# A softmax attention kernel: the place of small side matmuls within a key block is changed

## What is computed

```python
# layer 1: softmax attention, 16 heads of width 16, on n = layernorm(x)
q = n * rotation ; k = n * entangle ; v = n          # per head
out = softmax(q k^T / 4) v                            # 2048 x 2048 scores per head, 4*16 = 64 heads
# layer 2: token mixing with a shift by one token
r = sigmoid(xr W_r^T) ; kk = relu(xk W_k^T)**2 ; out = r * (kk W_v^T)
# layer 3: linear attention (feature maps of q and k, sums of K^T V), then a GELU feed-forward
# layer 4: silu(gate) * up feed-forward with integer weights
```

## Time and profile before

| | |
|---|---|
| median of 3 runs | 3122.75 us (3119.43 to 3122.9) |
| the profiled execution's own time | 3121.13 us |
| its span, first to last instruction | 3119.3 us |
| span of the attention stretch, first ACTIVATE to the last | 64.4 to 1985.9 us |
| granted TensorE clock, mean of the span | 0.986 |
| ACTIVATEs of scores | 2048, one for each half of each key block |

### The profile page before, as it was taken

The page is one execution under the profiler, slowest core; times in us unless marked ns, Lnnn a source line. Parts: engine busy times, 40 slices in busy tenths (PEclk is TensorE's granted clock), DMA queues, the critical chain, the costliest instruction groups (busy, mean ns, idle before and its releaser), DMA issues. The chain is left out here.

```text
span 3119.3 us, 48525 instructions
## 1 busy us (share of the span) xinstructions
PE 2872.7 (92%) x18320; PEld 1155.2 (37%) x18320; DVE 1400.0 (45%) x3422; ACT 2399.3 (77%) x2672; POOL 226.4 (7%) x194
## 2 busy tenths in 40 slices
PE   2999999999999999999999999579999999999996
PEld 0221221222222222222222222156666666666664
DVE  6231230322432233232430232276788888865675
ACT  2999999999999999999999999634444445543432
POOL 0000000000000000000000000011111112210110
PEclk9999999999999999999999999789999999999998
DMA  3411111310210211111211010121122212211110
GB/s 118 145 42 36 57 44 36 97 45 32 76 57 26 82 64 51 56 45 43 67 61 33 35 47 27 52 75 54 55 77 79 61 61 67 68 48 52 37 48 22
DMA packets 125586, 177.51 MB, mean 57 GB/s; under 512 B 42248, under 2 KB 100616, under 8 KB 125128
## 3 DMA queue, kind: packets, MB, share of 16 engines
q1 hardware_dynamic: 122392, 172.53, 17.1%
q10 hardware_dynamic: 2992, 2.23, 0.2%
HBM read 107.62 MB, written 67.11 MB: 56 GB/s over the span
## 5 line engine op out<-in xcount | busy, mean ns | idle before, releaser
L719 ACT ACTIVATE probs<-ps 128x1024 f32<-128x1024 f32 x2048 | 1893.0, 1168 | 66.2 <-PE ps L457 65.3
L580 PE MATMUL ps<-probs,vals 128*32 128x512 f32 x8192 | 1091.6, 605 | 2.8 <-ACT probs L719 2.8
L457 PE MATMUL ps<-qT,kT 64*128 64x512 f16 x4096 | 728.4, 385 | 89.6 <-DMA kT<-split_dram 23.8
L457 PEld LDWEIGHTS ps<-qT,kT 64*128 64x128 f16 x4096 | 173.2, 93 | 1130.7 <-ACT probs L719 1030.1
L580 PEld LDWEIGHTS ps<-probs,vals 128*32 128x32 f32 x8192 | 161.5, 108 | 294.0 <-issue 228.3
L874 DVE COPY sums<-ps 128x512 f32<-128x512 f32 x64 | 44.3, 692 | 500.8 <-PE ps L580 500.8
L1651 ACT ACTIVATE gate<-layers_ps 128x512 f32<-128x512 f32 x96 | 57.2, 595 | 251.5 <-DVE gated L1873 149.2
L1361 PE MATMUL layers_ps<-weight_mem,hT 128*128 128x256 f32 x1024 | 230.8, 380 | 0.0
L1361 PEld LDWEIGHTS layers_ps<-weight_mem,hT 128*128 128x128 f32 x1024 | 193.0, 190 | 29.9 <-ACT hT L1624 1.2
L1488 PE MATMUL layers_ps<-yT,weight_mem 128*128 128x512 f16 x768 | 173.4, 380 | 13.6 <-ACT hT L1624 13.6
L1514 PE MATMUL layers_ps<-n4T,weight_mem 128*128 128x512 f16 x768 | 175.1, 383 | 6.7 <-DVE y_out L1714 4.3
(11 more groups left out here) (237 smaller groups left out, 2603.5 us busy)
## 6 DMA issues: line engine op xcount, KB each, us to landing
split_dram<-parts SPq DMA_DIRECT2D x28, 768.0 KB, 3.7
qT<-split_dram SPq DMA_DIRECT2D x126, 128.0 KB
kT<-split_dram SPq DMA_DIRECT2D x126, 128.0 KB
heads_dram<-result SPq DMA_DIRECT2D x64, 128.0 KB, 7.3
q_in<-q_dram SPq DMA_DIRECT2D x16, 512.0 KB, 3.2
n_in<-n_dram SPq DMA_DIRECT2D x16, 512.0 KB, 3.5
x_in<-x_dram SPq DMA_DIRECT2D x16, 512.0 KB, 5.6
out_dram<-y_out SPq DMA_DIRECT2D x16, 512.0 KB, 4.3
```

Of the source, the lines that this page charges most:

```text
L457: last = nc.tensor.matmul(SCORES[slot][:, n * BANK:(n + 1) * BANK], kT[buf][rows, j * P:(j + 1) * P], qT[buf][rows, q0:q0 + BANK], start=T ...
L580: mm = nc.tensor.matmul(ACC[32 * c:32 * c + 32, :], vals[buf][:, j, :], probs[:, j % PROBS, c * BANK:(c + 1) * BANK], start=(j == 0), stop ...
L719: nc.scalar.activation(probs[:, j % PROBS, half * T // 2:(half + 1) * T // 2], SCORES[slot_of(at)], ACT.Exp, scale=OPERAND_SCALE ** -2).th ...
```

## The change

The lots of a front piece are issued behind S1 instead of between S0 and S1. The key block, the order of the two parts, all waits and all other work stay. The number of instructions is the same.

```diff
@@ -601,7 +601,7 @@ next_scores
                     half_scores(i % HALVES, slot_of(at), buf if i < HALVES else 1 - buf)
                     for part in range(2):
                         step = front_step(head, j - PART_GAP * part)
-                        if half == 0 and step is not None:
+                        if half == 1 and step is not None:
                             front(step, part, head, rounds_at(head, j - PART_GAP * part))
```

## The result

The changed kernel takes 3128.52 us (median of 16 runs, 3126.37 to 3132.33), the kernel before beside it 3122.82 us (16 runs, 3119.43 to 3124.77). The ratio is 1.0019, with a 95% interval of 1.0012 to 1.0027: slower by 5.7 us, between 3.7 and 8.4. The profiled execution has a span of 3126.4 us, 7.1 more than before.

A forecast was written before the change was run, and what follows sets the result against it. ScalarE, starved of scores, was taken to bound the attention. Uncovered waits less the saved switch, over 104 two-part lots (67 at +0.02, 24 at +0.20, 10 at +0.17, 3 at +0.09), gave 8.0 us: 3130.8, range 3127 to 3135.

The forecast's parts named there:

- ScalarE sets the pace, only its starvation counts: Attention stretch: ScalarE busy 1902.5 of 1921.9 us; TensorE's order matters only by moments when ScalarE has no scores.
- (a): S1 ahead of a lot: its wait, 0.30 us minus S0's lateness, is no longer covered by the lot.
- (b): TensorE's block with a lot: one change of operation saved, 0.09 us; lot to PV taken as 1.06 us.
- Every lot would lose 0.30, unrounded 0.29, whatever came before: Next S0 behind a two-part lot: 1.08 us late whatever came before, 0.78 bearable, so 0.30 lost (0.29 unrounded).
- (c): S1 comes earlier by up to the lot's length; nobody gains, as ScalarE stands still for the next S0.
- Transposing pieces cost nothing: The 16 transposing pieces: block lengthened by up to 0.61 us instead of 0.40, below 0.78, so nothing lost.
- VectorE's later read is covered: VectorE gets its bank 0.33 to 0.52 us later; nearest head end leaves 2.34 us of cover.
- R1: Rival, faster: S1's wait costs nothing, only the saved switch counts; 9.4 us go, 3113.4 us; chance 0.08.
- R2: Rival, slower: lot to PV dearer by 0.09 us, each lot costs its wait in full; 3140.1 us; chance 0.11.
- the first form of R3: Rival, no change: lot to PV cheaper by 0.09 us, 3121.4 us; chance 0.08 for both forms.
- The second form of R3: Rival: lot's loads start while S1 waits, hiding most of the wait; 3122.75 us or little below; 0.08 both forms.
- R4: Rival: VectorE's later reads delay the head's result or a turning round; 10 us above forecast, 3141 us; chance 0.03.

The follow-up runs named there:

- The lots at block 6: Part 1 moved from block 5 to 6 in heads without a turning round, against the kernel before: 3119.59 us between the halves, 3130.44 behind S1, against 3121.17.

## Why the prediction was right, point by point

The forecast was 3130.8 us, 8.0 more than before; measured are 5.7 (3.7 to 8.4), 7.1 in the profiled execution, on the side forecast and inside the narrow range of 3127 to 3135. The wide range, 3121 to 3140.5, also held "no change", so the time alone says little; what speaks for the prediction is that it came out lot by lot.

- *ScalarE sets the pace, only its starvation counts.* Held: the attention grew by 7.05 us and the losses at lots by 7.26.
- *(a) The wait is no longer covered.* Shown. The groups are 0.72, 0.87 and 0.90 long ahead of a lot, as forecast; moved alone, the first lots add 6.0 us of loss and the second ones 1.5; and only between the halves does a greater distance gain.
- *(b) One switch less saves 0.09, lot to PV is 1.06.* Shown: 1.06 (unrounded, the last record of a two-matmul lot to PV is 0.309, and to a half of scores it was 0.312). The saving is nearer 0.10, since 0.11 of wait lengthen the block by 0.01 only. This is the term that was mis-sized, a little: the 67 late lots changed by 0.012 instead of 0.02, the 24 steady ones by 0.19 instead of 0.20 and the 10 behind a quiet head end by 0.16 instead of 0.17, and some 0.01 at each of 104 lots is about the distance from 8.0 to 7.26. The sign at the 67 is a narrow thing: it is the difference of two nearly equal terms, 0.11 waited and 0.10 saved, and nearly all of the time comes from the other 37. Here the Trainium skill (TensorEngine Tiling (Array Packing), Key Properties), by which a change of tiling mode drains the array, agrees with the trace in kind: the changed order has one change of mode fewer and TensorE's part of the block, without the wait, is 2.60 instead of 2.70; the page names no price, so the "agrees in size" of the prediction was more than it allows.
- *Every lot would lose 0.30, unrounded 0.29, whatever came before.* Shown, with 0.28, except at the four group borders, which lose 1.06 and still change by the forecast amount.
- *(c) An earlier S1 helps nobody.* Nearly: at the group borders S1 had lost 0.40 to 0.41 and loses nothing now, but the next S0 loses 1.06 instead of 0.46, so the pair grows by 0.19, as in the sum.
- *Transposing pieces cost nothing.* Held: no loss at heads 26 to 28, 38 and 39 in either kernel.
- *VectorE's later read is covered.* Held in the change. The lots at block 6 show the cover's other end: in head 57 it was not there.
- *The rivals.* R1 (3113.4) needed a wait below 0.09 at the lots of blocks 5 and 13, and it is 0.11. R2 (3140.1) and the first form of R3 (3121.4) needed another step from lot to PV than 1.06. The second form of R3 needed the lot's loads to start while S1 waits: in all 64 lots of line 505 the first load starts 1 or 2 ns ahead of the lot's first matmul and 0.31 to 0.32 us behind the half of scores ahead of it, so none of the wait is used. R4 needed a new wait, and 73.0 of ScalarE's 73.3 us of idle time still come from the scores.

Open remains the distance from 7.1 in the traces to 5.7 in the medians. The one delay in head 47, 0.52 us in the profiled execution before and 0.06 in the changed one, has the other sign and does not explain it; the stretch behind the attention varies by up to 3.1 us among the profiled executions of these kernels (1130.9 to 1134.0), and the stretch ahead of it by 5.5 us (the first ACTIVATE of scores starts between 62.9 and 68.4). The change touches neither, so the length of the attention stretch is the sharper measure here, though of one execution each. The interval of the medians holds both 5.7 and 7.1, and no more was tried.

## What to carry to other kernels

In this kernel the engine that sets the pace is fed through a few buffers, and the wait of the filling engine for a free buffer is a slot in which side work costs nothing. Side work ahead of the waiting instruction is covered by that wait; behind it, the wait and the side work are both paid. Ahead of the instruction that the pacing engine needs next (S0 here) it is no better than behind: 7 us more. Read the length of the pair around the wait to see how large the slot is (0.30 us here). A late filler wins back one such wait in each block without side work, so the distance between pieces of side work counts as well as their place. Before moving side work later, look at what its consumers have queued behind it.

## What the runs showed of the hardware

The price of putting other work between like matmuls is steady: from the second matmul of a half to the next half without a wait 0.22 to 0.23 us, to a lot, a transposing piece or PV 0.31 to 0.32, at 2.4 GHz throughout (granted clock 1.00 in the attention stretch). And cutting a lot of four records in two costs 0.20 us, not 0.10. Besides the switch, the first two records behind a switch start 0.32 apart and the others 0.22: in the lot at 965.74 of the earlier trace rows the weights of the first record start to load together with its matmul, those of each later one about 0.21 us ahead of it, while the matmul before still runs.
